# x2 transposed in the mixers, four banks for the down projection, and the pieces of a decoder layer dealt out anew

## Chip, cores and metric

One core of a Trainium2 chip. The metric is device microseconds of one execution; lower is better. The kernel before takes 2867.22 us (median of 3 runs, 2864.83 to 2884.16).

## What is computed

One decoder layer in float32 on x of shape (32, 256, 256) with a context of the same shape: a selective state-space mixer, cross attention and eight experts, each with a residual and a layer norm behind it.

```python
def attn(x):                       # the state-space mixer
    xc, res = jnp.split(x @ W_in.T + b_in, 2, axis=-1)          # 2 x 512
    u = silu(causal_conv3(xc) + conv_b)
    dlt, Bm, Cm = jnp.split(u @ W_x.T, [64, 80], axis=-1)
    delta = softplus(dlt @ W_dt.T + b_dt)
    # per channel d (512), state n (16), in chunks of 64 tokens that start from 0:
    #   carry = exp(delta * A) * carry + delta * B * u ;  y = sum_n carry * C
    return (y * silu(res)) @ W_out.T + b_out
x = layernorm(x + attn(x))
# 16 heads of 16; softmax over the 256 context tokens
x = layernorm(x + cross_attention(x, ctx))
# eight experts, each 32 token columns of every batch (1024 tokens), inner size 704
x = layernorm(x + (silu(x_e @ w1_e) * (x_e @ w3_e)) @ w2_e)
```

## The kernel before

Two programs follow each other on the core: `mixers` (both attention parts, batch by batch) and `experts` (expert by expert). Each engine has one hand-ordered program; semaphores join them.

**The order of the work.** `run_steps` takes a list of (offset, piece) per engine. A step has 16 slots. A piece with offset o runs for batch b in step b + o // 16, in slot o % 16; within a slot the pieces run in the order of the list. So several batches are in flight: while batch b is scanned (offsets from O_SCAN = 17), batch b-2 is in its attention scores (O_S = 48) and batch b-4 in its output product (O_OF = 80). Every engine works strictly in that order, so a piece that waits holds up all that stands behind it. SyncE (SP) issues nearly all DMAs in such an order too; a wait before one DMA holds up the later ones.

**The scan.** The 512 channels with 16 states are cut in 16 tiles of 32 channels; a tile has 128 partitions (32 channels, 4 groups of states) by 4 states by 256 tokens. For tile t in slot t or next to it:
- SP replicates delta and w = delta * u from DRAM (`replicate(part)`, L362, four tiles a part, two buffers). They were stored there by `delta_store` (L343) and `w_store` (L347), and w was made by GpSimd (`w_piece`, L462).
- ScalarE makes the decays exp(delta * a) into one of three PSUM banks dA_ps, a half of the tile (two states) at a time (`decay`, L547).
- GpSimd makes dBu = w * B (`dBu_piece`, L471) into one of three buffers; it waits until the tile three before is scanned.
- VectorE scans each half (`scan`, L702). The result times C is hC. For the halves in HC_DVE VectorE scans in place in PSUM, multiplies (`hC_piece`, L715) and clears the first column of the bank (`clear_starts`, L725), and only this releases the bank and dBu. For the others GpSimd multiplies (`hC_piece`, L481): one full piece of 128x1024 for a tile with both halves, one of 128x512 for a single half.
- TensorE sums four tiles over the states (`state_sum`), VectorE multiplies with the gate (`gating`).

The lists of which half is whose, and the offsets:

```python
HC_DVE = [(1, 0), (1, 1), (2, 1), (3, 1), (4, 1), (6, 0), (6, 1), (8, 0), (9, 1), (10, 0), (10, 1)]
run_steps([
    (O_SP + 3, w_piece),
    *[(O_SCAN + t - 1, dBu_piece(t)) for t in range(NU)],
    *[(O_SCAN + t + 1, hC_piece(t)) for t in HC_POOL],
], B)
```

**Around it.** One PSUM bank, a_ps, serves conv, x_proj, half of dt, the output products, both transposes, q and k in turn (class `Bank`: the next writer waits for the last reader). v's projection goes to f_ps; VectorE adds the bias (`v_evac`, L764). The row maxima of the scores are transposed by TensorE and split in a high and a low part by VectorE (`max_parts`, L788 and L790), stored and loaded by ScalarE's queue as two more rows of q's stack. `residual` (L741 to L750) and `norm` (L557 to L568) run once after each attention part. q and k are stored to DRAM and loaded in stacks (`load_stack`, L403 and L405). The second norm's rows are stored by ScalarE (`store_x2`, L595), in the token order of the experts.

**The experts.** Two experts' weights and rows are held in what was the scan's memory (`Shared`). `load_experts` issues the first two on SP at O_S of the last batch; the last rows come behind the last store. Per expert of 1024 tokens: 16 transposes of 128x128 from rows to columns on TensorE (`transposes`, L1241, two banks t_ps), copied by ScalarE (`xT_evac`, L1138); 12 gate and 10 up products of 512 columns (`gate_up`, L1263), silu on ScalarE (L1152), the product hT on VectorE (L1178); eight down products (`down(t)`, t = 0 to 3, two each, L1281 and L1286) into two banks d_ps, each read by the residual on VectorE (L1198) and its statistics (L1201); then the norm (L1158, L1160, L1184, L1190) and four stores. The transposes for the next expert stand before `down(0)` and before `down(1)`.

## Time and profile before

| | |
|---|---|
| median of 3 runs | 2867.22 us (2864.83 to 2884.16) |
| profiled execution | 2879.43 us, span 2877.6 us |
| busy of the span | TensorE 2428.5 us (84%), VectorE 2197.8 (76%), GpSimd 2074.7 (72%), ScalarE 1782.2 (62%) |
| mean granted TensorE clock | 0.938 of full speed |
| DMA | 399.83 MB, mean 139 GB/s |

The span is from the first to the last instruction; the execution's own time is 1.8 us longer. Times in the profile are microseconds from the span's start, unless marked ns. PE is TensorE, DVE VectorE, ACT ScalarE, POOL GpSimd, SPq and ACTq the DMA issues of SyncE and ScalarE. An instruction's duration includes its latency, so one that follows without a gap starts before the other ends. In a row of waits the line after the arrow is the one that ended the wait. Helpers have one line for many operations (L843 for nearly every product), so these rows are told apart by their tiles.

### The profile page before, as it was taken

The page shows a single profiled execution, that of the slowest core. Times are in us where ns is not written, and L with a number is a line of the kernel's source. Part 1 is how long each engine was busy: PE and PEld are TensorE (multiplying, and loading weights), DVE is VectorE, ACT ScalarE, POOL GpSimd, SP SyncE. Part 2 cuts the span into 40 slices and gives each one's busy share as a digit, 9 for nine tenths or more (in the row PEclk, how much of TensorE's full clock was granted, in tenths as well). Part 3 has the DMA queues.
Part 4 walks back from the last instruction along what each step waited for, and adds up shares of the span by engine and source line. Part 5 has one row for each costly group of instructions (what it writes and reads, how often), then busy time and mean ns, then how long its engine had stood idle before and what let it go on. Part 6 is the DMA issues. An engine that isn't in the chain of part 4 may idle for free.

```text
span 2877.6 us, 49624 instructions
## 1 busy us (share of the span) xinstructions
PE 2428.5 (84%) x14784; PEld 1670.6 (58%) x14784; DVE 2197.8 (76%) x3746; ACT 1782.2 (62%) x3818; POOL 2074.7 (72%) x968
## 2 busy tenths in 40 slices
PE   4678888888888888888888888888886669999997
PEld 3355666666666666666666666666664445555554
DVE  1778999999999999999999999999998322222232
ACT  2566777777777777777777777777775332222221
POOL 2999999999999999999999999999998000000000
PEclk8788999999999999999999999999997769999999
DMA  4366666766666676667667666776774600322221
GB/s 134 100 151 157 160 160 162 169 161 171 177 175 166 170 172 159 161 173 167 156 161 160 165 164 164 172 173 163 170 168 111 161 27 15 104 65 62 62 62 30
DMA packets 258282, 399.83 MB, mean 139 GB/s; under 512 B 49921, under 2 KB 190593, under 8 KB 253922
## 3 DMA queue, kind: packets, MB, share of 16 engines
q1 hardware_dynamic: 238050, 376.72, 52.7%
q10 hardware_dynamic: 19968, 19.94, 2.5%
q8 instruction: 123, 2.02, 0.3%
q14 instruction: 141, 1.16, 0.2%
HBM read 301.06 MB, written 94.37 MB: 137 GB/s over the span
## 4 chain that ended last, share of the span: by engine, by line
PE 36%; POOL 17%; ACT 14%; issue 14%; DVE 10%; SPq 4%; DMA 3%; ACTq 1%; DVEq 0%; POOLq 0%
PE a_ps L843 12%; POOL arena L471 9%; POOL arena L481 8%; PE g_ps L1263 6%; PE d_ps L1281 5%; PE u_ps L1263 5%; ACT dA_ps L547 5%; PE f_ps L843 3%; DVE arena L702 2%; DVE dA_ps L702 2%; PE y_ps L843 2%; ACT probs L603 2%; SPq L403 1%; DVE mx L775 1%; PE s_ps L843 1%
## 5 line engine op out<-in xcount | busy, mean ns | idle before, releaser
L471 POOL TENSOR_TENSOR arena<-arena 128x1024 f32<-128x1024 f32 x512 | 1209.1, 2364 | 95.1 <-DVE dA_ps L725 74.0
L547 ACT ACTIVATE dA_ps<-arena,a_neg 128x252 f32<-128x252 f32 x2048 | 874.7, 465 | 178.1 <-DVE dA_ps L725 112.5
L702 DVE TENSOR_TENSOR_SCAN arena<-dA_ps,arena 128x512 f32<-128x512 f32 x672 | 805.3, 1207 | 115.6 <-ACT dA_ps L547 111.8
L481 POOL TENSOR_TENSOR arena<-arena 128x1024 f32<-128x1024 f32 (+1 forms) x416 | 808.0, 1942 | 17.0 <-DVE arena L702 17.0
L702 DVE TENSOR_TENSOR_SCAN dA_ps<-dA_ps,arena 128x512 f32<-128x512 f32 x352 | 425.5, 1216 | 10.5 <-POOL arena L471 6.3
L603 ACT ACTIVATE probs<-st_ps 128x512 f32<-128x512 f32 x512 | 301.3, 588 | 209.9 <-PE st_ps L843 203.6
L775 DVE TENSOR_REDUCE mx<-s_ps 128x2 f32<-128x512 f32 x512 | 343.9, 672 | 42.1 <-PE s_ps L843 40.9
L843 PE MATMUL a_ps<-xT,w_conv 128*128 128x256 f32 x1536 | 372.4, 393 | 0.0
L843 PE MATMUL s_ps<-k_st,q_st 96*128 96x256 f32 x1024 | 268.4, 344 | 91.1 <-DVE mx L775 69.1
L843 PEld LDWEIGHTS a_ps<-xT,w_conv 128*128 128x128 f32 x1536 | 290.5, 195 | 55.1 <-issue 16.7
L843 PE MATMUL y_ps<-arena,sel 128*32 128x256 f32 x4096 | 269.3, 406 | 45.3 <-POOL arena L481 42.3
L843 PEld LDWEIGHTS s_ps<-k_st,q_st 96*128 96x128 f32 x1024 | 168.7, 196 | 160.9 <-issue 122.0
L715 DVE TENSOR_TENSOR arena<-dA_ps,arena 128x512 f32<-128x512 f32 x352 | 230.8, 678 | 4.4
L843 PE MATMUL st_ps<-q_st,k_st 96*128 96x256 f32 x1024 | 215.9, 293 | 21.4 <-ACT probs L603 20.9
L843 PEld LDWEIGHTS y_ps<-arena,sel 128*32 128x32 f32 x4096 | 138.6, 117 | 161.7 <-POOL arena L481 71.5
L1178 DVE TENSOR_TENSOR hT<-silu,u_ps 128x512 f32<-128x512 f32 x80 | 55.0, 688 | 199.6 <-PE u_ps L1263 172.6
L1152 ACT ACTIVATE silu<-g_ps 128x512 f32<-128x512 f32 (+1 forms) x96 | 56.5, 596 | 215.0 <-PE g_ps L1263 214.9
L843 PEld LDWEIGHTS st_ps<-q_st,k_st 96*128 96x128 f32 x1024 | 164.4, 197 | 30.8 <-issue 19.9
L1263 PE MATMUL g_ps<-x2T,arena 128*128 128x512 f32 x384 | 181.8, 599 | 0.7 <-ACT x2T L1138 0.7
L843 PE MATMUL a_ps<-bias 2*128 2x512 f32 (+2 forms) x192 | 98.2, 512 | 90.5 <-ACT delta L537 24.6
L843 PE MATMUL f_ps<-probs,v 128*32 128x256 f32 x2048 | 153.6, 422 | 19.3 <-DVE v L764 18.6
L1281 PE MATMUL d_ps<-arena,hT 128*128 128x256 f32 x640 | 145.3, 382 | 15.7 <-DVE arena L1198 10.2
(107 smaller groups left out, 3243.0 us busy)
## 6 DMA issues: line engine op xcount, KB each, us to landing
arena<-delta_dram SPq DMA_DIRECT2D x512, 128.0 KB, 2.9
arena<-w_dram SPq DMA_DIRECT2D x512, 128.0 KB, 3.5
arena<-bc_dram SPq DMA_DIRECT2D x128, 256.0 KB, 4.6
q_st<-q_parts_dram SPq DMA_DIRECT2D x512, 64.0 KB
k_st<-k_parts_dram SPq DMA_DIRECT2D x512, 64.0 KB
w_dram<-u SPq DMA_DIRECT2D x32, 512.0 KB, 3.5
delta_dram<-delta SPq DMA_DIRECT2D x32, 512.0 KB, 4.2
k_parts_dram<-parts SPq DMA_DIRECT2D x32, 512.0 KB, 4.0
```

The costliest lines, as they stand in the source:

```text
L471: pool.tensor_tensor(dBu[:, n % NB], w_r[:, n // RP % 2, t % RP].unsqueeze(1).to_broadcast([P, QS, L]), bc_r[:, b.par, 0], ALU.mult).then_ ...
L481: pool.tensor_tensor(h[:, n % NH, states], h[:, n % NH, states], bc_r[:, b.par, 1, states], ALU.mult).then_inc(s_hC, 1)
L547: last = nc.scalar.activation(dA[n % NDA][:, q, :, 1:], delta_r[:, n // (2 * RP) % 2, t % RP].rearrange("p (c t) -> p c t", t=CH)[:, :, 1: ...
L603: nc.scalar.activation(probs[:, n % NPROB], st_ps[:], ACT.Exp, scale=float(DK) ** -0.5).then_inc(s_exp, 1)
L702: nc.vector.tensor_tensor_scan(dst, decays, dBu[:, n % NB, 2 * half:2 * half + 2].rearrange("p q t -> p (q t)"), 0.0, ALU.mult, ALU.add).t ...
L715: nc.vector.tensor_tensor(h[:, n % NH, 2 * half:2 * half + 2], state[:].rearrange("p q c t -> p q (c t)"), bc_r[:, b.par, 1, 2 * half:2 * ...
L775: nc.vector.tensor_reduce(mx[:, hd], s_ps[:], AX.X, ALU.max).then_inc(s_max, 1)
L843: return nc.tensor.matmul(out, lhsT, rhs, start=first, stop=last)
L1152: nc.scalar.activation(dst, g_ps[i % 2][first:last], ACT.Silu).then_inc(f_silu, 1)
L1178: nc.vector.tensor_tensor(hT[first:last, i // 2, HALF * (i % 2):HALF * (i % 2 + 1)], silu[first:last, i % 2], ups[first:last], ALU.mult).t ...
L1263: ins = nc.tensor.matmul(ps[i % 2][:], w13[:, b.par, k, col:col + P], x2T[:, k, cols], start=(k == 0), stop=(k == KD - 1))
L1281: nc.tensor.matmul(d_ps[i][:, 0:D], hT[:, k, tokens], w2[:, b.par, k], start=(k == 0), stop=False)
```

## The change

1. The halves whose hC VectorE makes go from eleven to nine, at other tiles. GpSimd then has 14 tiles instead of 13: nine in full, five by half.
2. v's bias comes from TensorE, as four rows of the product `bias`; ScalarE copies v (`v_evac`). The negated high part of the maxima is ScalarE's (`max_high`), VectorE keeps the low part (`max_low`).
3. x2 is transposed in the mixers, batch by batch (`transpose(r2, ...)` on TensorE at O_X2T = 94), copied by ScalarE (`x2T_evac`) and stored by SP in the column layout x2T_dram (`store_x2T`), 32 columns for each expert. The experts load columns (`load_columns`) instead of transposing. Of the last batch ScalarE copies the columns for experts 0 and 1 straight to their place. The first norm's and the second norm's rows get a tile each (x_tok, x1_tok).
4. The down projection has four PSUM banks (ND_PS), in place of the two of the transposes. A table load is asked for by name in the experts' norm.
5. Offsets and the order within slots change on all engines. The wait for VectorE's constants stands behind the first weight load instead of behind all of them.

```diff
-HC_DVE = [(1, 0), (1, 1), (2, 1), (3, 1), (4, 1), (6, 0), (6, 1), (8, 0), (9, 1), (10, 0), (10, 1)]
+HC_DVE = [(0, 1), (2, 1), (5, 1), (6, 0), (8, 0), (8, 1), (10, 0), (10, 1), (13, 1)]
...
-O_SILU = 8
+O_SILU = 9
-O_REP = 12
+O_REP = 14
-O_LD = 47
+O_LD = 48
-O_ONT = 78
+O_ONT = 79
-O_N2 = 80
+O_N2 = 85
+O_X2T = 94
...
                 for tile, name in weights:
                     sp.dma_start(tile, io[name]).then_inc(s_const, 16)
-                sp.dma_start(b_v[:], io["b_v"].partition_broadcast(P)).then_inc(s_const, 16)
-                sp.wait_ge(s_const_v, N_SET)
+                    sp.wait_ge(s_const_v, N_SET)
...
+            def store_x2T(b):
+                dst = shared.x2T_dram.rearrange("k e p t -> p (k e) t")[:, :, EC * b.c:EC * (b.c + 1)]
+                wait_all(sp, (s_x2T, 1, b, 1))
+                sp.dma_start(dst, x2T[:].rearrange("p k (e t) -> p (k e) t", t=EC)).then_inc(s_x2T_st, 16)
...
             run_steps([
-                (O_REP + 1, replicate(0)),
-                (O_XP + 2, bc_load),
-                (O_Q + 1, store_parts(q_dram, s_q_hi, s_q_lo, s_q_dram)),
-                (O_REP + 13, replicate(3)),
+                (O_OUT - 3, load_x_tok),
+                (O_Q + 2, store_parts(q_dram, s_q_hi, s_q_lo, s_q_dram)),
+                (O_S - 6, load_experts),
+                (O_REP + 5, replicate(2)),
+                *[(O_LD + HG * gr - 2, load_stack(gr)) for gr in range(NG)],
                 (O_SP + 1, w_store),
+                (0, load_x),
+                (O_REP + 4, replicate(1)),
+                (O_REP - 1, replicate(0)),
+                (O_XP + 1, bc_load),
+                (O_REP + 10, replicate(3)),
+                (O_OF - 1, load_x1),
+                (O_K + 4, store_parts(k_dram, s_k_hi, s_k_lo, s_k_dram)),
                 (O_SP + 1, delta_store),
...
+                (O_K - 4, load_ctx),
+                (O_X2T + 2, store_x2T),
             ], B)
...
             run_steps([
-                (O_SP + 3, w_piece),
                 *[(O_SCAN + t - 1, dBu_piece(t)) for t in range(NU)],
                 *[(O_SCAN + t + 1, hC_piece(t)) for t in HC_POOL],
+                (O_SP + 2, w_piece),
             ], B)
...
+            def v_evac(b):
+                act.wait_ge(s_v_mm, b.value(TT, TT))
...
+                nc.scalar.activation(v[:, b.par, :, :, 0:DK], f_ps[:].rearrange("p a (h i) -> p a h i", i=DK),
+                                     ACT.Copy).then_inc(s_v, 1)
...
+            def x2T_evac(b):
+                act.wait_ge(s_x2T_mm, b.value(1, 1))
...
+                if b.c == B - 1:
+                    for e in range(2):
+                        nc.scalar.activation(shared.x2T[:, e, :, ET - EC:], a_ps[:, :, EC * e:EC * (e + 1)],
+                                             ACT.Copy).then_inc(shared.last, 1)
+                nc.scalar.activation(x2T[:], a_ps[:], ACT.Copy).then_inc(s_x2T, 1)
...
             run_steps([
                 *[(O_E + hd, scores_T(hd)) for hd in range(H)],
+                (O_X2T, transpose(r2, s_x2, TT, s_x2T_mm, s_x2T, bank_a, a_ps)),
...
+                (O_XP, x_proj),
+                *[(O_DT, dt_proj(m)) for m in range(ND)],
+                *[(O_SCAN + 4 * m + 4, state_sum(m)) for m in range(ND)],
...
-                        if n >= 2:
-                            pe.wait_ge(f_r, b.value(EJ, n - 1))
+                        if n >= ND_PS:
+                            pe.wait_ge(f_r, b.value(EJ, n - ND_PS + 1))
...
-                *[(2 + 2 * part, transposes(part)) for part in range(KD)],
```

## Rows read from the trace of the kernel before

**Rows 1.** Windows: 25 steps, then five quiet ones; busy us (instructions) of each engine, clock, DMA.
```profile
core 0: us, PE busy (x) PEld busy (x) DVE busy (x) ACT busy (x) POOL busy (x), PEclk, DMA share, GB/s
415.50:2105.20 1689.70, 1462.12 (x10300) 1061.89 (x10300) 1591.93 (x2651) 1301.24 (x2851) 1612.10 (x751) 0.97 0.68 166
617.80:952.30 334.50, 290.82 (x2060) 210.72 (x2061) 318.37 (x533) 260.47 (x571) 322.79 (x151) 0.97 0.68 168
```

**Rows 2.** Groups by form, GpSimd: busy us, mean ns of one, idle before.
```profile
L471 POOL TENSOR_TENSOR arena<-arena 128x1024 f32<-128x1024 f32 x512 | 1209.1, 2364 | 95.1 <-DVE dA_ps L725 74.0 <-DMA arena<-w_dram 20.9
...
L481 POOL TENSOR_TENSOR arena<-arena 128x1024 f32<-128x1024 f32 x256 | 604.5, 2362 | 17.0 <-DVE arena L702 17.0
...
L481 POOL TENSOR_TENSOR arena<-arena 128x512 f32<-128x512 f32 x160 | 203.5, 1272 | 0.0
...
L462 POOL TENSOR_TENSOR u<-u,delta 128x1024 f32<-128x1024 f32 x32 | 75.5, 2360 | 41.6 <-ACT delta L537 41.6
```

**Rows 3.** Waits: who waited for whom, us in total, times, longest us.
```profile
POOL arena L471 <- DVE dA_ps L725: 74.0, 94, 3.9
...
POOL arena L471 <- DMA arena<-w_dram: 20.9, 17, 12.4
...
POOL arena L481 <- DVE arena L702: 17.0, 60, 2.3
...
PE d_ps L1281 <- DVE arena L1198: 10.2, 17, 0.6
```

**Rows 4.** Timeline of GpSimd in a quiet step: start us, us.
```profile
716.23 2.36 POOL L462 TENSOR_TENSOR u<-u,delta 128x1024 f32<-128x1024 f32 x1
...
730.53 2.35 POOL L481 TENSOR_TENSOR arena<-arena 128x1024 f32<-128x1024 f32 x1
732.84 2.37 POOL L471 TENSOR_TENSOR arena<-arena 128x1024 f32<-128x1024 f32 x1
```

**Rows 5.** Timeline of SyncE's DMA issues in the same step.
```profile
718.62 0.34 SPq L347 DMA_DIRECT2D w_dram<-u  x1
...
723.82 1.90 SPq L362 DMA_DIRECT2D arena<-delta_dram  x4
```

**Rows 6.** Timeline of GpSimd in a step whose replicated w came last.
```profile
1523.67 2.35 POOL L462 TENSOR_TENSOR u<-u,delta 128x1024 f32<-128x1024 f32 x1
1541.10 2.36 POOL L471 TENSOR_TENSOR arena<-arena 128x1024 f32<-128x1024 f32 x1 [0.76 <-DMA arena<-w_dram]
```

**Rows 7.** Groups by form, VectorE and ScalarE.
```profile
L715 DVE TENSOR_TENSOR arena<-dA_ps,arena 128x512 f32<-128x512 f32 x352 | 230.8, 678 | 4.4
...
L788 DVE TENSOR_SCALAR m_rows<-y_ps 8x128 fp32r<-8x128 f32 x128 | 32.8, 256 | 3.4 <-PE y_ps L986 3.4
...
L764 DVE TENSOR_TENSOR v<-f_ps,b_v_rows 128x512 f32<-128x512 f32 x32 | 21.3, 667 | 1.2 <-PE f_ps L843 1.2
...
L620 ACT ACTIVATE x1T<-a_ps 128x512 f32<-128x512 f32 x32 | 19.1, 597 | 12.8 <-PE a_ps L952 12.8
```

**Rows 8.** Timeline of TensorE in an expert, between the first two down products.
```profile
2473.53 1.09 PE L1241 MATMUL t_ps<-ident,arena 128*128 128x128 f32 x8
2474.46 4.48 PE L1281 MATMUL d_ps<-arena,hT 128*128 128x256 f32 x20
```

**Rows 9.** Chain that ended last, from mixers to experts: start us, us, what.
```profile
2354.55 0.31 ACTq L595
...
2359.68 3.91 PE t_ps L1241 x16
...
2364.26 3.78 PE g_ps L1263 x4
```

**Rows 10.** Timeline of TensorE at the start and in the last batch's scores.
```profile
15.02 0.79 PE L843 MATMUL a_ps<-bias 16*128 16x512 f32 x1 [15.02 <-DVE bias L680]
...
25.36 0.76 PE L843 MATMUL f_ps<-bias 4*128 4x512 f32 x1 [4.22 <-issue]
...
2296.74 0.80 PE L843 MATMUL s_ps<-k_st,q_st 96*128 96x256 f32 x2 [14.15 <-DMA q_st<-k_st]
```

**Rows 11.** The page's DMA queue of SyncE: packets, MB, share of 16 engines.
```profile
q1 hardware_dynamic: 238050, 376.72, 52.7%
```

More of the change, by code:

```diff
@@ L33 @@
 EJ = ET // P
+ND_PS = 4
 EPS = 1e-5
@@ L160, in load_rows, with load_columns @@
                      tokens.rearrange("a p j d -> (a p) j d")).then_inc(self.x[e % 2], 16)
+    def load_columns(self, sp, e, first, last):
+        src = self.x2T_dram.rearrange("k e p t -> e p k t")[bass.ds(e, 1), :, :, first:last]
+        sp.dma_start(self.x2T[:, e % 2, :, first:last],
+                     src.rearrange("a p k t -> (a p) k t")).then_inc(self.xT[e % 2], 16)
     def load_weights(self, sp, e):
@@ L241, in mixers @@
         onT = x1T
+        x2T = sb("x2T_batch", [P, KD, L])
         def bank(name, shape):
@@ L303, in mixers @@
         ]
-        N_WEIGHTS = len(weights) + 1
+        N_WEIGHTS = len(weights)
         N_CONV = 6 + NDA + TAPS * KD
@@ L1112, in load @@
                     return
+                wait_all(sp, (f_g_mm, 2 * FT, b.back(2), 2 * FT), (f_u_mm, 2 * FT - 2, b.back(2), 2 * FT - 2))
+                for first in range(0, ET, ET // 2):
+                    shared.load_columns(sp, b.c, first, first + ET // 2)
                 wait_all(sp, (f_out, 16 * OUTS, b.back(2), 16 * OUTS))
@@ L1124, in store @@
                     sp.dma_start(rows[q], x2[EC * q:EC * (q + 1), b.par]).then_inc(f_out, 16)
+            sp.wait_ge(shared.x2_st, 16 * B * OUTS)
+            for e in range(2):
+                shared.load_rows(sp, e, EJ - 1, EJ)
+            sp.wait_ge(shared.x2T_st, 16 * B)
             run_steps([(2 * SLOTS, store), (0, load)], E)
@@ L1131, in _ @@
             act.wait_ge(f_const_v, 1)
-            def xT_evac(b):
-                if b.back(1):
-                    act.wait_ge(f_g_mm, b.back(1).value(2 * FT, 2 * FT))
-                for i in range(2 * KD):
-                    act.wait_ge(f_t_mm, b.value(2 * KD, i + 1))
-                    nc.scalar.activation(x2T[:, i // 2, HALF * (i % 2):HALF * (i % 2 + 1)], t_ps[i % 2][:],
-                                         ACT.Copy).then_inc(f_t, 1)
             def gates(b):
@@ L1227, in _ @@
         def _(pe):
-            def transposes(part):
-                def piece(b):
-                    pe.wait_ge(f_x[b.par], b.same_parity(32))
-                    for i in (2 * part, 2 * part + 1):
-                        if i >= 2:
-                            pe.wait_ge(f_t, b.value(2 * KD, i - 1))
-                        else:
-                            if b.back(1):
-                                pe.wait_ge(f_t, b.back(1).value(2 * KD, 2 * KD + i - 1))
-                        k = i // 2
-                        for t in range(EJ // 2):
-                            ins = nc.tensor.transpose(t_ps[i % 2][:, t * P:(t + 1) * P],
-                                                      x2[:, b.par, EJ // 2 * (i % 2) + t, k * P:(k + 1) * P], ident[:])
-                        ins.then_inc(f_t_mm, 1)
-                return piece
             def gate_up(b):
-                pe.wait_ge(f_t, b.value(2 * KD, 2 * KD))
+                pe.wait_ge(f_xT[b.par], b.same_parity(32))
+                if not b.back(2):
+                    pe.wait_ge(shared.last, b.c + 1)
                 pe.wait_ge(f_w13[b.par], b.same_parity(64))
```

172 lines of the change are left out of this document (85 added, 87 removed).

## The prediction

> **What bounds the kernel now.** I read the windows first, then the costliest groups of GpSimd, then its waits. The window of [rows 1] from 415.5 to 2105.2 us holds 25 steps of the mixers (751 GpSimd pieces at 30 a step), so a step takes 67.6 us; the five quiet steps of the second row take 66.9. GpSimd is busy 1612.1 / 25 = 64.5 us of a step, VectorE 63.7, TensorE 58.5, ScalarE 52.0: two engines share the bound. [rows 2] give GpSimd's step: 16 products dBu, 8 full and 5 half products hC, one w, together 64.5 us. A full piece starts 2.31 us after the one before it ([rows 4], the last two), 2.33 with the mean of [rows 2] less the same overlap; a half costs 1.22. [rows 3] say what its idle time waits for: 74.0 us for VectorE's clearing of scanned banks, 17.0 for scans, 20.9 for the replicated w from DRAM, of which 12.4 is the first load. So 99.5 us of waits lie inside its run over 32 batches. The experts follow, bound by TensorE ([rows 8]).
>
> The chain that matters most to me is in [rows 4 to 6]. GpSimd makes w at 716.23; SyncE issues the two stores from 718.62 on, has them landed at 723.8, and issues the replicating loads; dBu of tile 0 needs them and starts at 732.84. Between the two GpSimd does w and six more pieces: 16.61 us, with 0.32 of a wait in it, so 16.3 of work. At 1523.67 the same chain ended last: 0.76 us of idle, 17.43 us from w to dBu ([rows 6], the longest of 14 such waits in the 25 steps). The loads land just as GpSimd comes to them.
>
> **The change, part by part.** *Nine halves on VectorE instead of eleven.* GpSimd gets 9 full and 5 half products where it had 8 and 5: one full piece more a batch, 64.5 + 2.33 = 66.8 us, or 32 x 2.33 = +74.6 us if its waits stayed. Nothing hides it: GpSimd is 95% busy.
>
> *VectorE lighter.* It loses two products of 0.60 us (0.677 less the overlap with the next), their memsets, v's bias (0.6) and four first halves of the maxima at 0.26 ([rows 7]): 2.9 us a batch, 63.7 to 60.8. In a step of 67 or more that is 9% of slack instead of 5%, while GpSimd has none. GpSimd's waits for VectorE (91.0 us, 2.8 a batch) come from two queues of equal load that run three buffers apart. They can fall to nothing or stay as they are; I take 0.6 a batch, 19 us, nearer nothing, since VectorE is relieved by as much as the waits amount to.
>
> *The chain of w.* The new halves also make the second half of tile 13 VectorE's. Its product lies between w and dBu(0), so GpSimd's work there falls from 16.3 to 16.3 - (2.33 - 1.22) = 15.2 us. The position of w in GpSimd's order is unchanged (after dBu(12)), and so is SyncE's order of w store, delta store, q store, replication; the ctx load only passes ahead of the q store, and both are issued before the stores have landed. If the loads land 16.6 us after w, GpSimd stands 1.4 us in each step: 31 x 1.4 = 43 us. Bounds: no stall when the chain shrinks to 15.2 (x_proj now stands ahead of a state sum, so the load of B and C may be earlier and leave the queues free); 2.2 us, 69 in all, at 17.43. I take 1.4, from the step in which the loads were just in time.
>
> So GpSimd's waits go from 99.5 to 43 + 19 = 62, and the scanned part costs 74.6 - 37.5 = +37 us. Bounds: waits of 10 (-15 us) and of 99.5 + 43 (+118).
>
> *More on ScalarE and TensorE.* ScalarE gets v's and x2T's copies, 0.6 us each ([rows 7]), and four small negations of about 0.25: 52.0 becomes 54.2. TensorE gets four transposes and one bias product, 0.6 + 0.5 us. Both stay below 61 of 67 us, hidden under GpSimd; without that cover they cost the chain through bank a_ps at most their own 1.7 us. Silu comes a slot later, x1T's copy a slot earlier, and x_proj needs both: I cost the pair at nothing. The stack loads come one slot later, the scores don't: their cover is a slot of 4.2 us, and TensorE has 8 us of slack a step.
>
> *Start.* Nine weight loads now wait for VectorE's constants, done about when TensorE's first product starts (15.02). The first gate product, which needs all weights, ran at 25.36 ([rows 10]). 2.0 MB at the 166 GB/s of [rows 1] from 15.3 on are there at 27.4: +2 us (0 to +4).
>
> *Experts.* TensorE waits 17 times for the residual before it reuses a bank, 10.2 us ([rows 3]), with 0.06 of hand-over each: 11.2 us. With four banks a bank is asked for again two pairs later, over 10 us, so nothing is late next. The second eight transposes of an expert hold the products up by 2474.46 - 2473.53 = 0.93 us ([rows 8]), seven times: 6.5. The first eight stand in the wait for the last product of hT, so they bring nothing. Sum -17.7 us (-11 to -18). The columns are loaded two experts ahead. Of the two table loads in the norm one goes, the other moves behind the same wait: 0 (to -1.3 at the very end).
>
> *Between the stages.* Before: stores, rows loaded, 3.91 us of transposes, copy, gate at 2364.26, 9.7 us after the stores began at 2354.55 ([rows 9]). After: transposes 1.1, ScalarE's four store issues beside them 1.75, copies 1.0, SyncE's store of x2T (in its program ahead of the last column loads) 0.5, two loads, 3 to land: 6.3. That is -3.4 us. But batch 30's transposes and copy now stand before batch 31's output product: +2. And the experts' weights (with 1.8 MB of columns more) are issued before the stacks of batch 30's last heads and of batch 31; before, batch 31's second group waited for them, 14.15 us ([rows 10]). The same flood moves forward; TensorE stands earlier and has eight slots to do behind it: +5 (-5 to +12). Sum +3.6.
>
> **Sum.** 37 + 2 - 17.7 + 3.6 = +25 us. The profiled execution took 2879.4 us (span 2877.6), so it would take 2904. It stands 12 us above the median of the runs shown; I put the same difference on the median: 2867.2 + 25 = 2892 us, +0.9%. About 1% is what a measurement of this kernel can tell from no change.
>
> **Rivals.** (A) GpSimd runs without waits, because the w chain gets shorter too and VectorE is never late. Waits of 10 us: 74.6 - 89.5 - 12.1 = -27 us, 2840. For it: the relief of VectorE. Against it: the chain would have to land at 15.2 us in every step, and [rows 4, 6] show 16.6 and 17.4.
>
> (B) GpSimd's waits for VectorE stay, since they come from single late tiles (the residual, ScalarE's table loads) and not from the mean load. Place: dBu(t) waits for the scan of tile t-3. It decides from 0.7 us a batch upwards, where +1% is passed. With half of the 91 us kept the sum is +51, 2919; with all kept and the stall partly inside them (112 us of waits) +75, 2942. I take 2920.
>
> (C) The store of x2T is cut in runs of 32 columns, 128 bytes: 2048 packets a batch. No row shows such a packet alone. By the mean packet of [rows 11], 0.527 x 16 x 2877.6 / 238050 = 0.102 us, it is 13 us of each of 16 DMA engines a step, and the DMA share goes from 0.68 to 0.87; by its bytes 1.5 us and 0.70. At the upper figure the replication and stack loads behind it are late, and a step costs some 1.5 us more: 32 x 1.5 = +48 on top, 2940. Against it: it is issued in slot 0, when w's chain is over. The Trainium skill (DMA: Bandwidth & Descriptors, Specifications) says that a transfer wants at least 512 B for full rate and that below this the engine reads, modifies and writes. By that rule this store sits at the dear end and C is its case; the sum above leaves it out.
>
> (D) Four banks don't act, another wait takes the place of the residual's: -17.7 becomes 0, 2910.
>
> **How the numbers follow.** Forecast 0.45, A 0.15, B 0.22, C 0.10, D 0.08. The forecast's own spread (chain of 15.2 to 17.4 us, start, tail) is 2855 to 2915. Slower by over 1% (above 2896): B, C, D and a little of the forecast: 0.42. Faster by over 1% (below 2838.5): about half of A and little else: 0.12. Within 1%: 0.46. The range that leaves 2 in 10 outside goes from 2843 to 2932.
>
> **What would show it.** A step of 68.5 to 69.2 us, GpSimd busy 66.8 of it. The wait of dBu for the replicated w in nearly every step, 1 to 2 us each, 30 to 60 in total; the wait for the cleared banks under 30 us. VectorE busy near 61 a step. Experts at 60.0 us instead of 62.2, no wait for the residual before a down product. The first gate product of expert 0 some 6 us after the last norm. I am wrong if a step is under 67.5 (the chain shortened, A), if the clearing still ends most waits (B), or if TensorE waits for stacks in the steady steps (C).

## The result: 53 us slower, and the profile after

The changed kernel takes 2928.76 us (median of 4 runs, 2923.93 to 2936.83), the one before 2875.69 on the same chip (2864.83 to 2885.52): a ratio of 1.0186, 95% interval 1.0163 to 1.0209. I had forecast 2892, no change to be told; the time lies within the range given, but the change is clear of noise. The profiled execution took 2931.59 us with a span of 2929.6, 52.0 more than the span of before.

Where the span went, by stages. GpSimd's first dBu stands at 70.6 us instead of 67.7, its last at 2297.4 instead of 2217.4, so the scanned part got 77.1 us longer. TensorE's first gate product of the experts is at 2433.13 us instead of 2364.26 [rows 9]: from the last dBu 135.7 us instead of 146.9, 11.1 less. The experts take 496.5 us instead of 513.3, 16.9 less. The line of GpSimd's dBu (count, ns min/median/max, first and last start), the window of the experts and the chain of waits into them:

```profile
L488 POOL TENSOR_TENSOR arena<-arena x512: 2332/2359/2420, 70.6 to 2297.4; 128x1024 f32<-128x1024 f32 x171
```
```profile
2433.13:2929.60 496.47, 471.08 (x1472) 262.58 (x1472) 143.36 (x336) 81.04 (x128) 0.00 (x0) 0.98 0.24 71
```
```profile
2429.59 3.50 DMA arena<-x_columns
2433.13 3.78 PE g_ps L1283 x4
```

A window of the mixers after, some 24 steps (761 GpSimd pieces at 31 a step), then four steps from one w to the next (columns as in [rows 1]):

```profile
428.20:2148.10 1719.90, 1545.81 (x10210) 1105.92 (x10210) 1503.86 (x2376) 1314.69 (x2942) 1632.17 (x761) 0.92 0.67 163
...
673.30:747.50 74.20, 68.17 (x417) 48.58 (x415) 60.24 (x94) 53.23 (x121) 66.69 (x32) 0.84 0.65 155
...
1104.00:1171.80 67.80, 58.42 (x418) 41.91 (x417) 61.12 (x97) 53.75 (x121) 66.60 (x32) 1.00 0.71 170
...
1655.70:1723.90 68.20, 60.82 (x417) 43.78 (x417) 61.22 (x98) 53.52 (x121) 66.63 (x31) 0.95 0.71 169
...
1935.20:2006.70 71.50, 65.45 (x417) 46.68 (x417) 61.44 (x98) 53.54 (x121) 66.72 (x31) 0.88 0.65 157
```

Over the 26 steps from the w at 392.0 us to that at 2218.9 the mean is 70.3 us (67.6 before). Nine take 69.0 or less, most of them 68.2 to 68.8, thirteen 70.9 or more, most of them 71.5. GpSimd's busy time is the same 66.7 in each; what differs is TensorE, 58 to 68 us busy with the same products, at a mean granted clock of 1.00 to 0.84. (x_proj runs slow, some 3.5 us for eight products instead of 1.9, in steps of both lengths, 21 of 32 in all. The eight q products take 3.65 us in the step at 819 and 1.99 in that at 1656; they take more than 2.6 us in 23 of 32 batches, in none before.) Before, the clock moved too, and the steps with it, but less:

```profile
649.60:716.20 66.60, 56.60 (x413) 41.27 (x412) 63.70 (x108) 52.10 (x115) 64.46 (x31) 1.00 0.69 174
...
1594.60:1664.00 69.40, 62.41 (x414) 44.90 (x413) 63.72 (x108) 52.08 (x115) 64.52 (x32) 0.90 0.70 161
```

The waits after (us in total, times, longest), to be held against [rows 3]:

```profile
POOL arena L488 <- DMA arena<-w_dram: 77.3, 30, 12.1
POOL u L479 <- ACT delta L554: 49.5, 17, 42.9
POOL arena L498 <- DVE arena L752: 32.8, 45, 2.2
POOL arena L488 <- DVE dA_ps L775: 4.2, 14, 0.8
...
PE a_ps L874 <- ACT u L533: 62.0, 32, 4.8
```

The clearing of banks (74.0 before) is gone; the replicated w has taken its place, 77.3 of which 12.1 is the first load. GpSimd has 2.33 us a batch more to do (75 us) and waits in its run a little longer than before: 65.2 + 6.6 + 32.8 + 4.2 = 109 us, where [rows 2, 3] with the same first waits left out give 8.5 + 1.9 + 17.0 + 74.0 = 101. The last row is new: x_proj now stands ahead of the state sum and waits for ScalarE's silu. One step, GpSimd and then SyncE's issues:

```profile
819.05 2.35 POOL L479 TENSOR_TENSOR u<-u,delta 128x1024 f32<-128x1024 f32 x1 [0.50 <-ACT delta L554]
...
836.94 2.35 POOL L488 TENSOR_TENSOR arena<-arena 128x1024 f32<-128x1024 f32 x1 [2.31 <-DMA arena<-w_dram]
```
```profile
821.43 0.34 SPq L357 DMA_DIRECT2D w_dram<-u  x1
...
826.43 0.34 SPq L389 DMA_DIRECT2D ctxT<-in_ctxT  x1
827.00 0.37 SPq L397 DMA_DIRECT2D q_parts_dram<-parts  x1
827.53 2.36 SPq L372 DMA_DIRECT2D arena<-delta_dram  x4
829.93 0.42 SPq L372 DMA_DIRECT2D arena<-w_dram  x1
```

From w to dBu(0) it is 17.9 us. The ctx load waits for v_proj (31 times in the run, 137.5 us of SyncE's idle time) and stands ahead of replicate(0), which is issued at 827.53, 6.1 us after the w store; before it was 5.2 [rows 5].

### The profile page after: what moved, and what is told of

It reads as the page before. It is cut to its first block, busy times and chain, and to the rows that moved or that the text cites. A ratio compares the mean times of both kernels' runs of the same rounds, so it can differ in the third digit from the quotient of the medians.

```text
span 2929.6 us, 49716 instructions
## 1 busy us (share of the span) xinstructions
PE 2543.6 (87%) x14816; PEld 1734.8 (59%) x14816; DVE 2122.4 (72%) x3458; ACT 1804.5 (62%) x3972; POOL 2144.5 (73%) x1000
## 3 DMA queue, kind: packets, MB, share of 16 engines
q1 hardware_dynamic: 308306, 393.30, 53.9%
## 4 chain that ended last, share of the span: by engine, by line
PE 56%; POOL 13%; issue 11%; ACT 10%; DVE 6%; SPq 2%; DMA 1%; ACTq 1%; DVEq 0%; POOLq 0%
PE a_ps L874 23%; PE f_ps L874 7%; POOL arena L488 7%; PE g_ps L1283 6%; POOL arena L498 6%; PE d_ps L1301 5%; PE u_ps L1283 5%; PE y_ps L874 4%; PE s_ps L874 2%; ACT dA_ps L564 2%; DVE arena L752 2%; PE st_ps L874 1%; ACT L533 1%; DVE dA_ps L752 1%; ACT gate L528 1%
## 5 line engine op out<-in xcount | busy, mean ns | idle before, releaser
L488 POOL TENSOR_TENSOR arena<-arena 128x1024 f32<-128x1024 f32 x512 | 1207.9, 2361 | 81.6 <-DMA arena<-w_dram 77.3
L752 DVE TENSOR_TENSOR_SCAN arena<-dA_ps,arena 128x512 f32<-128x512 f32 x736 | 878.2, 1209 | 139.6 <-ACT dA_ps L564 132.8
L498 POOL TENSOR_TENSOR arena<-arena 128x1024 f32<-128x1024 f32 (+1 forms) x448 | 884.8, 1975 | 33.1 <-DVE arena L752 32.8
L874 PE MATMUL s_ps<-k_st,q_st 96*128 96x256 f32 x1024 | 283.6, 360 | 76.9 <-DVE mx L816 62.5
L752 DVE TENSOR_TENSOR_SCAN dA_ps<-dA_ps,arena 128x512 f32<-128x512 f32 x288 | 345.3, 1209 | 0.0
L874 PEld LDWEIGHTS a_ps<-xT,w_conv 128*128 128x128 f32 x1536 | 289.5, 195 | 54.6 <-issue 16.6
L874 PE MATMUL y_ps<-arena,sel 128*32 128x256 f32 x4096 | 255.5, 391 | 32.4 <-POOL arena L498 28.6
L874 PEld LDWEIGHTS s_ps<-k_st,q_st 96*128 96x128 f32 x1024 | 180.3, 203 | 163.8 <-issue 130.0
L874 PE MATMUL st_ps<-q_st,k_st 96*128 96x256 f32 x1024 | 220.2, 298 | 20.7 <-ACT probs L627 16.6
L874 PEld LDWEIGHTS y_ps<-arena,sel 128*32 128x32 f32 x4096 | 128.1, 112 | 152.3 <-issue 55.0
L765 DVE TENSOR_TENSOR arena<-dA_ps,arena 128x512 f32<-128x512 f32 x288 | 190.1, 677 | 3.4
L1283 PE MATMUL g_ps<-arena 128*128 128x512 f32 x384 | 181.8, 599 | 5.5 <-DMA arena<-x_columns 5.5
L1301 PE MATMUL d_ps<-arena,hT 128*128 128x256 f32 x640 | 146.5, 384 | 11.6 <-issue 10.1
L1283 PE MATMUL u_ps<-arena 128*128 128x512 f32 x320 | 150.9, 594 | 0.0
```

The lines of the kernel that those rows point to most:

```text
L488: pool.tensor_tensor(dBu[:, n % NB], w_r[:, n // RP % 2, t % RP].unsqueeze(1).to_broadcast([P, QS, L]), bc_r[:, b.par, 0], ALU.mult).then_ ...
L498: pool.tensor_tensor(h[:, n % NH, states], h[:, n % NH, states], bc_r[:, b.par, 1, states], ALU.mult).then_inc(s_hC, 1)
L752: nc.vector.tensor_tensor_scan(dst, decays, dBu[:, n % NB, 2 * half:2 * half + 2].rearrange("p q t -> p (q t)"), 0.0, ALU.mult, ALU.add).t ...
L765: nc.vector.tensor_tensor(h[:, n % NH, 2 * half:2 * half + 2], state[:].rearrange("p q c t -> p q (c t)"), bc_r[:, b.par, 1, 2 * half:2 * ...
L874: return nc.tensor.matmul(out, lhsT, rhs, start=first, stop=last)
L1283: ins = nc.tensor.matmul(ps[i % 2][:], w13[:, b.par, k, col:col + P], x2T[:, b.par, k, cols], start=(k == 0), stop=(k == KD - 1))
```

## The experiments

Eighteen kernels. "Before" was measured again beside each group: 2878.2, 2875.8, 2876.3, 2876.7, 2875.4 us. Numbers are medians; the theories are numbered in the order in which they came up. Differences between two kernels are between their medians, and those of some 5 us or less are within the noise.

### First group: the slots and the halves, one at a time

**e1_ctx**, load_ctx behind replicate(0) in SyncE's list:
```
-                (O_K - 4, load_ctx),
+                (O_K - 2, load_ctx),
```


> The changed kernel with one edit: SyncE's load_ctx, which waits for v_proj and stood in slot 11 ahead of the q store and replicate(0), goes to slot 13 behind them. The changed kernel stands 53 us above the one before (2928.8 against 2875.7 us). Theory 1 (the wait of SyncE for v_proj, 4.4 us a batch, makes the loads of w late; dBu(0) stood 65 us for them): the wait of dBu for the replicated w falls from 77 to under 35 us, a step falls from 70.3 to about 69.2 and the time by 30 to 40 us, to 2889 to 2899. Theory 2 (the chain of w is late because x_proj stands ahead of the state sum and because ScalarE's silu is a slot later): the wait stays above 55 us and the time is within 12 us of the changed kernel. Theory 3 (the additional GpSimd piece is the whole loss): within 5 us of the changed kernel, dBu's wait gone or not.

2971.5 us, 43 slower. All theories missed, though the edit did what it should:

```profile
POOL arena L498 <- DVE arena L752: 121.4, 125, 3.8
...
POOL arena L488 <- DMA arena<-w_dram: 13.9, 6, 12.2
...
PE a_ps L874 <- DMA ctxT<-in_ctxT: 65.0, 29, 4.0
```

The wait for w is gone but for its first 12.2 us. But k_proj now waits 65 us for ctx, and the scans are late instead (121.4 for 32.8). So the load of ctx is pulled both ways: w's replication wants it later, k_proj earlier. That k_proj's wait is what makes the scans late is my reading.

**e2_silu**, silu back and x_proj behind the state sums:
```
-O_SILU = 9
+O_SILU = 8
@@ tensor
-                (O_XP, x_proj),
                 *[(O_SCAN + 4 * m + 4, state_sum(m)) for m in range(ND)],
+                (O_XP, x_proj),
```


> The changed kernel with silu back in slot 8 and x_proj behind the state sums in TensorE's list, as before. Theory 2 (x_proj waits for silu with nothing else issued behind it, TensorE stands 2 us, its clock drops and everything up to w and the q products is late): TensorE's wait for silu (62 us) goes to under 10, the steps of 71.6 us at a clock of 0.88 go, all stand at 68.3 or less, the time falls by 30 to 50 us to 2879 to 2899. Theory 1 (SyncE's wait for v_proj makes w late): the wait of dBu for w keeps over 55 us and the time is within 12 us of the changed kernel's. Theory 3 (the additional GpSimd piece is the whole loss): within 5 us.

3031.1 us, 102 slower. TensorE's wait for silu went, but silu with its two table loads (4.6 us) now stands in slot 8 ahead of the second decay in the new list of ScalarE; VectorE's scans in dA_ps wait 104.5 us for decays, up to 4.1 at a time, where the changed kernel's wait 0.0.

**e3_halves11**, HC_DVE as before:

> The changed kernel with the eleven halves of hC on VectorE as before; all else changed. Theory 3 (GpSimd is the bound, the additional full piece of 2.33 us a batch costs its whole length): 75 us less, about 2854 to 2865, under the kernel before. Theories 1 and 2 (the late chain of w sets the step, GpSimd only stands in it): GpSimd's work falls by 2.33 us a step but its wait for w grows from 65 to 100 us or more, since the pieces between w and dBu(0) are then less of a limit than the loads; the time falls by 20 to 45 us, to 2884 to 2909.

2912.7 us, 16 less: a smaller gain than any theory gave, and 34.6 us above the kernel before. The halves are the smaller part of the loss.

**e4_oldorder**, halves, slots and the lists of all engines as before; the rest of the change kept:

> The eleven halves, the slots and the order of the pieces on every engine as before, with the other parts of the change kept: x2 transposed in the mixers (slot 94), four banks, v's bias on TensorE, v and the high parts of the maxima on ScalarE, the weight loads behind VectorE's constants. If the loss lies in the new dealing of slots and halves (theories 1, 2 and 3 alike): the experts take 60.0 us each (-17 us), the scanned part is as before or, with VectorE relieved, up to 25 us less, start +3: 2834 to 2866. If the small packets of the x2T store or the additional work on ScalarE and TensorE cost something themselves (theory 4): 2876 or more.

2965.7 us, 88 above before with the order of before. So the parts I had priced at nothing cost, in this order, more than the halves. One step shows it, on ScalarE, VectorE and TensorE:

```profile
1020.76 1.28 ACT L533 ACT_TABLE_LOAD   x1
1022.06 1.06 ACT L533 ACTIVATE u<-u 128x1024 f32<-128x1024 f32 x1
1023.02 1.04 ACT L535 ACTIVATE gate<-gate 128x1024 f32<-128x1024 f32 x1
1024.08 1.28 ACT L536 ACT_TABLE_LOAD   x1
1025.37 0.27 ACT L665 ACTIVATE m_rows<-y_ps 8x128 fp32r<-8x128 f32 x1
...
1025.67 0.28 DVE L822 SCALAR_TENSOR_TENSOR m_rows<-y_ps,m_rows 8x128 fp32r<-8x128 f32 x1 [4.04 <-ACT m_rows L665]
...
1026.10 3.64 PE L874 MATMUL y_ps<-arena,sel 128*32 128x256 f32 x32 [3.31 <-DVE m_rows L822]
```

A 0.27 us negation stands behind 4.6 us of silu and table loads; VectorE stands 4.04 us for it with its scans queued behind, and the state sum, which needs the same bank y_ps, 3.31 us.

### Second group: one part at a time onto the kernel before

**f1_x2T_only**: the kernel before with x2T in the mixers, the separate x1_tok, load_columns, ND_PS = 4.

> The kernel before with one part of the change: x2 transposed in the mixers (copy on ScalarE in slot 94, its store behind the other transfers, columns loaded by the experts, a separate buffer for x1) and four banks for the down products. Eleven halves, slots, order, v and the maxima on VectorE and the start as before. Kernel e4_oldorder, with v and the high maxima on ScalarE besides, took 2965.7 us, and its VectorE stood 126.5 us for ScalarE's high maxima, its TensorE 101.1 us for the low ones. Theory 5 (the handing over of the maxima between ScalarE and VectorE costs the scanned part some 100 us in the old order): this one loses them all: experts -17 us, tail some -5 to -11, scanned part 0 to +10: 2850 to 2868. Theory 4 (x2T's transposes, copy or its 2048 packets a batch disturb the mixers): 2885 or more, with steps longer than 67.6 us and no wait for maxima.

2850.9 us, ratio 0.9902 (0.9882 to 0.9922): the best of all. It stores 2048 small packets a batch more, and in the list of waits no engine of the mixers waits for that store; the most common step is 66.6 us. SyncE's queue goes from 52.7% [rows 11] to 54.1% here, and on the page of the changed kernel to

```profile
q1 hardware_dynamic: 308306, 393.30, 53.9%
```

**f2_nine**: the kernel before with the new HC_DVE.

> The kernel before with the nine halves of the changed one and nothing else. In the changed kernel, going from eleven to nine took 16 us (2912.7 to 2928.8 us) where the additional full piece is 74.6 us of GpSimd. Theory 6 (GpSimd's waits of 99.5 us absorb most of it, as its waits for VectorE go): +15 to +45 us, 2891 to 2923, with GpSimd's wait for the cleared banks under 30 us instead of 74.0. Rival (the old order is tight, GpSimd's waits stay): +60 to +80 us, 2936 to 2956. The forecast on record had this part at +37.

2916.8 us, +41, as theory 6 has it. GpSimd's waits:

```profile
POOL u L462 <- ACT delta L537: 44.3, 6, 39.7
POOL arena L481 <- DVE arena L702: 38.4, 40, 3.8
POOL arena L471 <- DMA arena<-w_dram: 31.6, 22, 11.7
POOL arena L471 <- DVE dA_ps L725: 0.9, 3, 0.4
```

Waits in the run: 4.6 + 38.4 + 19.9 + 0.9 = 64 us, where the forecast had 62.

**f3_v_act**: f1_x2T_only with v on ScalarE and TensorE, and the stricter start.

> f1_x2T_only with v's bias on TensorE and v's copy on ScalarE (and the weight loads behind VectorE's constants, +2 to +4 us); the maxima stay on VectorE. Between this kernel and e4_oldorder stands only the hand-over of the maxima. Theory 5: the maxima are the price, v is not: within 10 us of f1_x2T_only, 90 us or more under e4_oldorder's 2965.7. Rival (the work moved to ScalarE and TensorE costs wherever it is): half of the distance between f1_x2T_only and e4_oldorder or more.

2860.4 us, +9.6, theory 5: in the order of before, v costs little, and the maxima 105 (to e4_oldorder).

**f4_neworder**: f1_x2T_only in the new order.

> The changed kernel with eleven halves, and with v and the maxima wholly on VectorE and the start as before: what is left of the change is x2T in the mixers, four banks, and the slots and orders dealt out anew. Against f1_x2T_only it shows the new order by itself, against e3_halves11 (2912.7 us) the moved v and maxima in the new order. Theory 7 (the new order is itself slow: silu a slot later, x_proj ahead of the state sum and waiting for silu, 62 us of TensorE's idle time, the chain of w late): 2895 to 2930, and slower than f1_x2T_only by 30 us or more. Rival (the new order is good and only serves to hide the hand-over): within 12 us of f1_x2T_only, and the changed kernel's loss is then the offloaded parts.

2871.6 us, 21 above f1_x2T_only and 41 under e3_halves11. Both theories have a part: the new order costs 21 by itself and saves 53 once the maxima are shared (e4_oldorder to e3_halves11).

### Third group: queue position, banks, start

**g1_silu9**, e4_oldorder with `O_SILU = 9`:

> e4_oldorder (order of before, maxima shared out) with one number changed: silu in slot 9 instead of 8, where it stands behind the high maximum of the second group in ScalarE's list. In e4_oldorder ScalarE does silu with its two table loads (4.6 us) ahead of that 0.27 us negation; VectorE stood 4.04 us for it and TensorE's state sum 3.31 us more, once a batch. Theory 8 (this one queue position is the price of the shared maxima in the old order, 105 us between f3_v_act, 2860.4, and e4_oldorder, 2965.7): TensorE's wait for the low maxima falls from 101 to under 25 us, the time by 60 to 100 us, to 2866 to 2906. Rival (each of the four hand-overs costs by itself, through the shared bank y_ps): the time stays within 25 us of 2965.

2938.7 us, 27 of the 105. TensorE's wait for the low maxima falls from 101.1 to 1.2 us, and the time by only a quarter of the price: x_proj now waits 84.4 us for silu, and w for delta 47 us beyond the first time (23 in e4_oldorder).

**g2_max_dve**, the changed kernel with max_parts on VectorE again:

> The changed kernel with one part undone: the maxima wholly on VectorE again (nine halves, new order, v on ScalarE, silu in slot 9 as in the change). Theory 9 (of the 41 us that moving v and the maxima to ScalarE and TensorE costs in the new order, 2871.6 to 2912.7, most is the maxima: VectorE waits for ScalarE four times a batch, 27 us, and ScalarE's row of tasks gets longer just before silu): 2888 to 2908, 20 to 40 us less than the changed kernel. Rival a (v is the price: its copy waits on ScalarE for v_proj, 48.7 us in e3_halves11, and holds the decays up): within 10 us of the changed kernel. Rival b (neither counts once GpSimd has nine halves): within 5 us.

2926.0 us, 3 less: with v moved, the maxima cost next to nothing (rival b).

**g3_two_banks**, f1_x2T_only with `ND_PS = 2`:

> f1_x2T_only (2850.9 us) with two banks for the down products instead of four. The forecast on record: TensorE's waits for the residual cost 10.2 + 1.0 us, so +11 us, 2862. The rival on record (four banks don't act): 2851 as with four. If the removed transposes were what TensorE needed to hide the residual: more than +11.

2868.2 us, +17. From the first gate product (2353.14) to the end it takes 513.7 us, as long as before the change (513.3).

```profile
PE d_ps L1298 <- DVE arena L1230: 16.1, 24, 0.7
```

10.2 us in 17 waits were with the transposes [rows 3]; without them it is 16.1 in 24.

**g4_v_start**, f3_v_act with the weight loads ahead of `sp.wait_ge(s_const_v, N_SET)`:

> f3_v_act with the weight loads issued ahead of VectorE's constants as before (one wait less strict); v stays on TensorE and ScalarE. In f3_v_act the first dBu starts at 73.5 us instead of 65.0 in f1_x2T_only, and from there to the last hC it takes 2.3 us less. Theory 10 (the start is the whole difference of 9.6 us between the two): 2849 to 2854, first dBu at 65 to 66 us. Rival (v's copy costs the steady steps): 2858 to 2862, first dBu at 65 all the same.

2854.9 us: the start costs 5.5 of the 9.6 us, v's move 4, which is hardly to be told from nothing.

### Fourth group: silu, x_proj, the clock

**h1_silu9_alone**, f1_x2T_only with `O_SILU = 9`:

> f1_x2T_only (2850.9 us, order of before) with silu in slot 9 instead of 8, nothing else. The forecast on record cost this at nothing: 2846 to 2856. Theory 11 (x_proj waits for silu each batch, some 2 us, and delta, w and all behind them come later by as much; GpSimd's wait for delta appears, 47 us of it in g1_silu9 beyond the first): 2872 to 2905, TensorE's wait for u at 60 us or more, steps of 68 us instead of 66.6.

2939.2 us, +88 for one slot, where I expected +21 to +54. The waits (f1_x2T_only has 65.9, 38.9, 49.9 for the first three):

```profile
POOL arena L491 <- DVE dA_ps L756: 119.4, 91, 4.0
POOL u L482 <- ACT delta L557: 77.8, 32, 39.5
...
DVE mx L806 <- PE s_ps L874: 143.7, 58, 20.4
...
PE a_ps L874 <- ACT u L536: 93.7, 30, 3.5
```

TensorE stands 3 us a batch for silu with the scores in its queue behind; VectorE stands for the scores with the scans behind; GpSimd stands for the cleared banks. Read so, one wait of the engine with slack is handed through two queues to the engine without; the waits fit this, no run takes one link out.

**h2_xproj_back**, the changed kernel with x_proj behind the state sums:

> The changed kernel with x_proj behind the state sums, as before; silu stays in slot 9. So TensorE has the state sum (2 us) to do while ScalarE is at silu. Theory 12 (TensorE's idle 1.74 us ahead of x_proj costs the time, by itself and through the clock): TensorE's wait for u falls from 62 to under 15 us, the clock rises from 0.906 to 0.93 or more, 2880 to 2915. Rival (x_proj comes 0.3 to 4 us later in the chain to w, and what counts is the chain): 2929 to 2980, the wait of dBu for w or of w for delta longer than 77 and 50 us.

2949.7 us, +21: x_proj's place is right, given silu in slot 9.

**h3_filler**, the changed kernel with
```
+                for k in range(5):
+                    mm(a_ps[0:RANK + 2 * NS, 0, :], w_x[:, k % ND], w_q[:, k % KD], True, True)
                 pe.wait_ge(s_u, b.value(1, 1))
```


> The changed kernel with five products of constants (128x96 by 128x256) ahead of x_proj's wait for silu, into the bank that x_proj overwrites: work without a use that fills TensorE's idle 1.74 us. Theory 13 (the clock is a cause: after the idle time it is granted low, x_proj takes 3.5 us instead of 1.9, and the step becomes 71.6 instead of 68.3): x_proj at about 2 us, clock above 0.93, most steps at 68.3, the time 30 to 60 us lower, 2869 to 2899. Rival (the clock only comes with the long steps): TensorE has 2 us more to do in each step and the time stays at 2925 or rises to 2960.

2930.6 us, no change. In the trace the 32 x_proj take 1.92 us in the mean, the longest 2.60; in the changed kernel 21 of 32 take over 3 us (2.99 in the mean of all). So filling the time ahead of x_proj takes its slow level away, and the slow x_proj by itself is not what the time hangs on. The idle time alone doesn't decide the level: in the changed kernel 28 of the 32 have the same 1.74 us ahead of them, and ten of those are fast. And the filler doesn't show what the clock as a whole costs. The low level only went elsewhere: v_proj takes more than 2.6 us in 10 batches (6 in the changed kernel), the q products in 25 (23), k_proj in 18 (26). The granted clock over the whole of a run is 0.915 to 0.924 in the fast ones, hardly above the changed kernel's 0.906 to 0.919, and TensorE has 2.4 us a batch more to do.

**h5_new_nine**, f4_neworder with nine halves:

> f4_neworder (2871.6 us: new order, v and maxima on VectorE, start as before) with nine halves. Against the changed kernel it lacks only v and the maxima on ScalarE and TensorE and the stricter start. Theory 14 (nine halves cost +41 where nothing else is late, as in f2_nine, and the moved work then adds only what the start costs, 5 us, and v 4): 2908 to 2920. Rival (the moved work is the loss, in the nine-halves kernel too, through TensorE's bias product and ScalarE's longer row): 2880 to 2895.

2876.1 us, under both expectations, and decisive. It is the changed kernel without v and the maxima moved and with the start of before, and as fast as the kernel before. Nine halves cost 4.5 us here.

### Fifth group: which half of v

**k1_v_copy_dve**, the changed kernel with v's copy as a tensor_copy on VectorE:

> The changed kernel with v's copy on VectorE (a plain copy behind k's low part); the bias product stays on TensorE. Theory 15 (v_proj ends some 1.3 us later on TensorE, by the bias product and by the lower clock; SyncE's ctx load waits for it and stands ahead of replicate(0), so w's replication is issued 7.8 us after the w store instead of 6.5 and dBu(0) is late by as much each batch): the copy's engine does not matter, 2912 to 2940. Theory 16 (the copy is the price: 0.6 us and a wait for v_proj ahead of the decays in ScalarE's list): 2875 to 2895.

2935.2 us: v's copy on VectorE gives nothing back.

**k2_v_dve**, the changed kernel with v as before:

> The changed kernel with v as before (bias and copy in one VectorE instruction, start as before); the shared maxima, nine halves, new order stay. Against the changed kernel (2928.8) it shows what v costs, against h5_new_nine (2876.1) what the shared maxima cost. Theories 15 and 16 alike: v is the loss, 2874 to 2890. Rival (either move alone brings the kernel to its slow level, since GpSimd has no slack left): 2910 to 2930.

2889.9 us: v is 39 of the loss (some 5 of it the start, by g4_v_start's pair), the maxima 14 where v stays as it was. The other way round, v is 50 where the maxima stay (h5_new_nine to g2_max_dve) and the maxima 3 on top; the sum of 53 is the same. The 14 is the less sure: ten runs from 2877.8 to 2900.1 us against twelve of h5_new_nine from 2870.1 to 2883.1. Between k1_v_copy_dve and k2_v_dve, 45 us apart, stand the bias product of 0.5 us ahead of v_proj and the start. One step of h5_new_nine and one of g2_max_dve, SyncE:

```profile
1007.57 0.34 SPq L360 DMA_DIRECT2D w_dram<-u  x1
...
1010.61 0.34 SPq L392 DMA_DIRECT2D ctxT<-in_ctxT  x1
...
1014.04 2.87 SPq L375 DMA_DIRECT2D arena<-w_dram  x4
```
```profile
1011.32 0.34 SPq L357 DMA_DIRECT2D w_dram<-u  x1
...
1015.66 0.34 SPq L389 DMA_DIRECT2D ctxT<-in_ctxT  x1
...
1019.15 1.81 SPq L372 DMA_DIRECT2D arena<-w_dram  x4
```

From the w store to the replication of w 6.5 us and 7.8 us; in the mean the two kernels are only 0.6 us apart. Averaged over 26 steps of each timeline, from the start of w on GpSimd to the end of v_proj on TensorE and to the issue of w's replication; then GpSimd's waits in its run (the first load left out) for the replicated w and for VectorE, and the time from the first dBu to the last, all us:

| kernel | end of v_proj | w replicated | waits for w | for VectorE | first to last dBu | time |
|---|---|---|---|---|---|---|
| before | 5.9 | 9.7 | 8.5 | 91.0 | 2149.7 | 2875.7 |
| f1_x2T_only | 5.9 | 9.6 | 5.4 | 81.1 | 2139.6 | 2850.9 |
| h5_new_nine | 6.5 | 10.1 | 43.5 | 17.6 | 2183.1 | 2876.1 |
| k2_v_dve | 6.5 | 10.2 | 37.7 | 40.0 | 2202.5 | 2889.9 |
| g2_max_dve | 7.0 | 10.7 | 59.4 | 26.1 | 2209.8 | 2926.0 |
| k1_v_copy_dve | 7.3 | 11.1 | 47.8 | 57.6 | 2233.6 | 2935.2 |
| after | 7.5 | 11.3 | 65.2 | 37.0 | 2226.8 | 2928.8 |

The waits for w and for VectorE of h5_new_nine and of k2_v_dve are in these rows:

```profile
POOL arena L491 <- DMA arena<-w_dram: 56.1, 32, 12.6
...
POOL arena L501 <- DVE arena L733: 15.6, 34, 1.5
```
```profile
POOL arena L491 <- DMA arena<-w_dram: 50.3, 26, 12.6
...
POOL arena L501 <- DVE arena L747: 32.5, 52, 2.5
```

In the last five kernels of the table, all with nine halves in the new order, the scanned part is longer by what GpSimd waits more (2.5 to 6.6 us for delta counted in), to some 2 us. The two moves don't arrive by the same way. The shared maxima alone (h5_new_nine to k2_v_dve) lengthen it by 19.4 us, and it is the waits for VectorE that grow, by 22.4; w's replication isn't later. v's move (k2_v_dve to after) lengthens it by 24.3 us; the waits for w grow by 27.5, with the replication issued 1.1 us later a step. The rest of the 33 us between these two traces is the first dBu, 5.8 us later, and 3.5 us behind the last.

That the ctx load is the only carrier of v's cost is not shown. e1_ctx, which took it out of the way, was slower for another reason. g2_max_dve has the replication only 0.6 us later than h5_new_nine, 19 us in all, and stands 50 us above it (34 between the two traces), with 8.5 us more of waits for VectorE; in k1_v_copy_dve most of the increase over k2_v_dve is for VectorE too. In the order of before the ctx load stands behind the q store, and that waits 94.1 us for VectorE in the kernel before, so v_proj's end matters less there (f3_v_act: w replicated at 9.8, and v costs 4 us).

The bias product is not all that makes v_proj end late. The q products stand ahead of it in TensorE's list. In the changed kernel they run at the lower level in 20 of the 26 steps, and there v_proj ends at 7.8; in the other six it ends at 6.3. In k2_v_dve it is 6.9 in 17 and 5.8 in nine. So the bias product goes with some 0.5 us, 0.9 where the clock is low, and slow q products with 1.2 to 1.6 more. In all nine kernels with the order of before every batch's eight q products take 2.0 us.

## Why the forecast was wrong

The way from before to after, each step one of the kernels above: x2T and four banks -24.9 (f1_x2T_only), the new order +20.8 (f4_neworder), nine halves +4.5 (h5_new_nine), shared maxima +13.8 (k2_v_dve), v with the start +38.9 (after). Sum +53.1. By the steps of the forecast:

- **Nine halves, +37**: right for the kernel before (+41, waits of 64 us for a forecast of 62), with luck in the split: 39 from VectorE for 19, and 20 from w for 43. The halves together with the new order and without the moved work (h5_new_nine) come out as the text had them: waits of 43.5 for w and 17.6 for VectorE, steps of 68.7 us, the scanned part 33 longer. But I put the wait for w down to the halves alone, and eleven halves in the new order have 33 of it already. Added to the new order, nine halves are +4.5, because f4_neworder's GpSimd already stood 125 us in its run (73.8 - 39.3 for delta, 45.3 - 12.1 for w, 40.7 and 17.0 for VectorE) and h5_new_nine's 64. The added work took the place of waits.
- **More on ScalarE and TensorE, "hidden under GpSimd"**: this is the step that failed, with some 47 us of the loss (53 with the start): that much lies between h5_new_nine, 2876.1, and the changed kernel, 2928.8. I compared busy times (54 and 61 of 67 us) and so asked whether the engine is full, not who stands in its queue. The runs show two costs in its place. The shared maxima make scans late (waits for VectorE 17.6 to 40.0 us). With v's bias product v_proj ends later, and the loads of w behind it in SyncE's list too (waits for w 37.7 to 65.2). The text had the ctx load passing ahead of the q store and called it harmless since "both are issued before the stores have landed". They are not: the load waits 4.4 us a batch for v_proj, and in the step shown the two are issued 5.0 and 5.6 us (821.43 to 826.43 and 827.00) after the w store, where before the stores had landed after 5.2 [rows 5].
- **"Silu comes a slot later ... I cost the pair at nothing"**: failed. Alone it is +88 us (h1_silu9_alone). With shared maxima it is the better place: in slot 8 the second high maximum stands behind silu (e4_oldorder, +105), and slot 9 gives 27 of that back (g1_silu9); in the new order slot 8 is 81 us worse (e2_silu against h2_xproj_back). With x_proj, the gates and the decays moved around it, the new order as a whole costs 21; how much of that is silu's isn't shown.
- **Start, +2**: the first gate product ran at 30.8 us for 25.4 [rows 10], the first dBu 2.9 us later; 5.5 us in the time of g4_v_start's pair.
- **Experts, -17.7**: -16.9. The sum was right and its split was not. Two banks without the transposes take as long as before (513.7 us), so taking the transposes out of a kernel with two banks brought 0 and not 6.5: the waits for a bank went from 17 to 24 and from 10.2 to 16.1 us; the seven new ones are, as I read it, where transposes had stood between. Four banks then brought 16.6 (513.7 to 497.1 in f1_x2T_only).
- **Between the stages, +3.6**: -11.1. The new order drains faster: from the last dBu to the end 628.4 us in f4_neworder, 646.8 in f1_x2T_only. It gives back 17 of the 37 us that its steps lose.
- **The step, 68.5 to 69.2**: nine of 26 steps are at or near it; 71.5 was in no case of mine.

The rivals. A and D didn't occur. B came nearest in time (2920). Of the 91 us of waits for VectorE 37 stay, nearer B's half than my 19; but it is the moved work that brings 19 of them (17.6 in h5_new_nine), and most of the loss stands elsewhere, so B's time is luck in the main. Its sign, the clearing, fell from 74.0 to 4.2 us. C, the small packets, is false here: the DMA share of the steps is 0.67 for 0.68 [rows 1], the queue's 52.7% became 53.9 and f1_x2T_only is faster by 25 us. 70256 packets more took 1.2 points of the queue's share, and no wait for that store shows in the mixers. The Trainium skill (DMA: Bandwidth & Descriptors, Specifications) puts the least transfer for full rate at 512 B; no run here shows what a single packet of 128 B costs.

What stays open: whether TensorE's lower clock makes the long steps or comes with them. Steps and clock go together in both kernels, and so do the runs of one program: of k2_v_dve's ten, the shortest took 2877.8 and 2878.1 us at a mean granted clock of 0.936 and 0.939, the longest 2898.0 and 2900.1 at 0.924 and 0.918. Slow q products do make v_proj end later, yet in the changed kernel the steps up to such a w are only 0.8 us longer in the mean. h3_filler took the slow level out of x_proj and left it in half of the k_proj and more of the others, and the time stayed. Open too is how v's cost splits between the ctx load and the rest, and what else of the +105 the shared maxima carry in the order of before. f1_x2T_only beats both kernels and is the one to keep.

## What to carry to other kernels

Moving an instruction of half a microsecond to an engine with slack need not be free (v's move cost 4 us in one order and 39 or more in the other): look at what is queued behind it and ahead of it in each in-order list, DMA issues included, and who holds those. Put the parts of a bundle on the old kernel one at a time: here one part (-25 us) was worth having and was hidden by others that cost 78. Savings and costs that use the same idle time don't add: going from eleven halves to nine costs 41 us on the kernel before and 4.5 in the new order.

## What the runs showed that I had not expected

One slot of one ScalarE piece moves the kernel by 88 us (3%); as the waits read, through three in-order queues. TensorE's clock is not one number of a kernel: its mean over a step goes from 0.84 to 1.00 of 2.4 GHz. Eight products of x_proj take 3.5 us (the lower level, 1.2 GHz) in 21 of 32 batches, most of them after 1.74 us of idle time, and 1.9 us (the higher) in nearly all of them once useless products fill that time; but then more of the q and v products are slow.
